# Scatters of a mixture of experts that wait tile by tile

## The reference

```
x = x + attention_like(conditioning(x, fside))      # two-way recurrences, gates, W_out
x = x + mixture_of_experts(conditioning2(x, fside)) # what this case is about
```

```
probs = softmax(xr @ Wg);  gate_vals, expert_idx = top_k(probs, 2)
h = relu(einsum('ecd,edf->ecf', dispatched, w1))    # 512 -> 2048
expert_out = einsum('ecf,efd->ecd', h, w2)          # 2048 -> 512
out[row] = sum over its two experts of gate * expert_out
```

## Time and profile before

| what | us |
|---|---|
| median of 3 runs | 1220.02 (1217.79 to 1220.59) |
| profiled execution, its device time | 1219.18 |
| its span, first to last instruction | 1217.1 |
| PE busy | 1039.4 (85% of the span) |
| PEld busy | 827.9 (68%) |
| DVE busy | 677.7 (56%) |
| ACT busy | 533.8 (44%) |
| POOL busy | 322.6 (27%) |
| PE clock granted, mean | 0.953 of full |

### The profile page before, as it was taken

One profiled execution on the slowest core, in us unless ns is written; L12 is line 12 of the kernel. 1 busy time (PEld: TensorE's weight loads), 2 busy tenths in 40 slices (PEclk: granted clock), 3 DMA queues, 4 the chain that ended last, 5 costly groups with the idle time before them and its releaser, 6 DMA issues.

```text
span 1217.1 us, 17595 instructions
## 1 busy us (share of the span) xinstructions
PE 1039.4 (85%) x5058; PEld 827.9 (68%) x5059; DVE 677.7 (56%) x970; ACT 533.8 (44%) x914; POOL 322.6 (27%) x251
## 2 busy tenths in 40 slices
PE   1146797787799829999999999999999999999994
PEld 0022344344348529998999899989898888999883
DVE  6989899899781523334333433355555344343553
ACT  5455746826844212334333433344545334333453
POOL 3878818648630330001100200020201101100302
PEclk9998998997999759999999999999999999999998
DMA  5251340211010452113421621282535234322711
GB/s 191 104 166 35 122 133 35 69 70 69 0 71 35 174 175 104 69 69 118 106 69 69 149 76 69 69 220 91 186 138 186 83 132 134 87 69 69 216 70 21
DMA packets 63406, 125.29 MB, mean 103 GB/s; under 512 B 4726, under 2 KB 4762, under 8 KB 63384
## 3 DMA queue, kind: packets, MB, share of 16 engines
q1 hardware_dynamic: 54728, 107.91, 25.6%
q0 software_dynamic: 8656, 17.13, 7.0%
HBM read 93.04 MB, written 35.22 MB: 105 GB/s over the span
## 4 chain that ended last, share of the span: by engine, by line
PE 58%; issue 1%; ACT 1%; DVEq 1%; DVE 1%; POOL 0%; ACTq 0%; POOLq 0%
PE ps_y L1137 10%; PE ps_y L1138 10%; PE ps_y L1139 10%; PE ps_h L1117 9%; PE ps_h L1119 9%; PE ps_h L1118 9%; PE ps_t L1087 1%; POOL out_dram L1066 0%; ACT xh L1232 0%; ACT y L1239 0%; DVEq L1177 0%; DVE hl L1294 0%; ACT w1h L1204 0%; DVE w1l L1255 0%; ACTq L1177 0%
## 5 line engine op out<-in xcount | busy, mean ns | idle before, releaser
L1117 PE MATMUL ps_h<-xh,w1h 128*128 128x320 f32 (+3 forms) x768 | 247.6, 322 | 7.9 <-issue 4.0
L1119 PE MATMUL ps_h<-xh,w1l 128*128 128x320 f32 (+3 forms) x768 | 243.6, 317 | 0.0
L1118 PE MATMUL ps_h<-xl,w1h 128*128 128x320 f32 (+3 forms) x768 | 243.5, 317 | 0.0
L1066 POOL DMA_INDIRECT out_dram<-y,token x40 | 64.6, 1615 | 657.6 <-ACT y L1239 487.7
L1294 DVE SCALAR_TENSOR_TENSOR hl<-ps_h,hh 128x320 fp32r<-128x320 f32 (+1 forms) x192 | 106.9, 558 | 194.0 <-ACT hh L1228 185.3
L1137 PE MATMUL ps_y<-w2h,hh 128*128 128x512 f32 x528 | 206.5, 391 | 1.9 <-DVE hl L1294 1.9
L1138 PE MATMUL ps_y<-w2h,hl 128*128 128x512 f32 x528 | 206.7, 391 | 0.0
L1139 PE MATMUL ps_y<-w2l,hh 128*128 128x512 f32 x528 | 206.1, 390 | 0.0
L1258 DVE TENSOR_TENSOR w2l<-raw,w2h 128x512 fp32r<-128x512 f32 x128 | 88.6, 692 | 196.5 <-ACT w2h L1207 193.6
L1228 ACT ACTIVATE hh<-ps_h 128x320 fp32r<-128x320 f32 (+1 forms) x192 | 94.4, 492 | 232.4 <-PE ps_h L1119 232.2
L1207 ACT ACTIVATE w2h<-raw 128x512 fp32r x128 | 80.7, 631 | 211.2 <-PE ps_y L1139 210.2
(11 more groups left out here) (194 smaller groups left out, 1290.4 us busy)
## 6 DMA issues: line engine op xcount, KB each, us to landing
raw<-in_L_ffn_w_dram SPq DMA_DIRECT2D x64, 1024.0 KB
slots<-r_rows SPq DMA_DIRECT2D x8, 1302.5 KB, 16.1
rows<-slots SPq DMA_DIRECT2D x8, 1302.5 KB
f_rows<-in_fside_BxSxS_dram SPq DMA_DIRECT2D x5, 1024.0 KB, 5.3
rows<-in_x_dram SPq DMA_DIRECT2D x4, 1024.0 KB, 6.4
out_dram<-x_rows SPq DMA_DIRECT2D x4, 1024.0 KB, 4.9
slots<-r_rows POOLq DMA_DIRECT2D x1, 1302.5 KB
rows<-slots SPq DMA_DIRECT2D x5, 260.5 KB, 4.1
```

Of the source, the lines that this page charges most:

```text
L1117: nc.tensor.matmul(o, w1h[:, j, dt, :], xh[:, dt, lo:hi], start=(dt == 0), stop=False)
L1118: nc.tensor.matmul(o, w1h[:, j, dt, :], xl[:, dt, lo:hi], start=False, stop=False)
L1119: last = nc.tensor.matmul(o, w1l[:, j, dt, :], xh[:, dt, lo:hi], start=False, stop=(dt == CT - 1))
```

## The change

Every eviction now raises its engine's semaphore by one. The thresholds are scaled: `Y_EVEN` = 3 even tiles and `Y_ODD` = 2 odd tiles per expert. In a narrow expert, whose tile 4 has no eviction, ScalarE's eviction of tile 2 adds 2. GpSimd waits, ahead of scatter i, for the count that tile i's eviction reaches; the wait for `s_y0` (y has been cleared) comes first. TensorE and VectorE wait for the same events as before, under the new thresholds.

```diff
+    Y_EVEN, Y_ODD = (ST + 1) // 2, ST // 2
...
-            pool.wait_ge(s_ya, e + 2)
-            pool.wait_ge(s_yv, e + 2)
             pool.wait_ge(s_y0, 1)
-            pool.nop(nofuse=True)
             for i in range(ST):
+                if i % 2 == 0:
+                    pool.wait_ge(s_ya, Y_EVEN * (e + 1) + i // 2 + 1)
+                else:
+                    pool.wait_ge(s_yv, Y_ODD * (e + 1) + i // 2 + 1)
+                pool.nop(nofuse=True)
                 pool.indirect_dma_start(
...
-                    pe.wait_ge(s_ya, e + 1)
-                    pe.wait_ge(s_yv, e + 1)
+                    pe.wait_ge(s_ya, Y_EVEN * (e + 1))
+                    pe.wait_ge(s_yv, Y_ODD * (e + 1))
...
-        act.sem_inc(s_ya, 1)
+        act.sem_inc(s_ya, Y_EVEN)
...
                 for i in range(0, ST if wide else ST - 1, 2):
-                    last = a.activation(y[:, i], ps_y[:, i, :], ACT.Copy, scale=gate[:, i:i + 1])
-                last.then_inc(s_ya, 1)
+                    a.activation(y[:, i], ps_y[:, i, :], ACT.Copy, scale=gate[:, i:i + 1]).then_inc(
+                        s_ya, 2 if i == ST - 3 and not wide else 1)
...
-        dve.sem_inc(s_yv, 1)
+        dve.sem_inc(s_yv, Y_ODD)
...
-            dve.wait_ge(s_ya, e + 1)
-            dve.wait_ge(s_yv, e + 1)
+            dve.wait_ge(s_ya, Y_EVEN * (e + 1))
+            dve.wait_ge(s_yv, Y_ODD * (e + 1))
...
                 for i in range(1, ST if wide else ST - 1, 2):
-                    last = v.tensor_scalar(y[:, i], ps_y[:, i, :], gate[:, i:i + 1], None, ALU.mult)
-                last.then_inc(s_yv, 1)
+                    v.tensor_scalar(y[:, i], ps_y[:, i, :], gate[:, i:i + 1], None, ALU.mult).then_inc(s_yv, 1)
```

## The result

The changed kernel takes 1216.76 us (median of 22 runs, 1215.48 to 1219.51), the kernel before 1218.95 (22 runs, 1217.45 to 1220.93). Ratio 0.9985, 95% interval 0.9978 to 0.9992: faster, by 1.0 to 2.7 us, so the gain is clear of the noise though it is only 0.2%. Forecast were 1218.8 us and a gain of 1.2.

What follows compares the result with a forecast made beforehand. TensorE was taken to bound the expert stage and GpSimd's scatters the tail. The first scatter's 1.19 us, all other terms 0, off the 1220.02 us median gave 1218.8 us, range 1217.2 to 1220.7.

Steps and rivals of the forecast that it cites:

- What bounds it, and that only the tail counts: Whole kernel: TensorE alone sets the expert stage, GpSimd's five scatters the end from 1203.2 us; only there can time be gained.
- The wait of 648 us: Experts' first scatters waiting for evictions, 487.7 us behind ScalarE and 160.2 behind VectorE; nearly all idle time beside 728 us of matmuls.
- The first scatter, 1.19 us: Last expert: waiting for tile 0 alone, GpSimd starts scattering at 1202.02 us in place of 1203.21, 1.19 us earlier.
- Scatters two to five: Last expert: each follows at a pitch of 1.86 us with its tile ready; none waits again.
- the added waits: Four more waits and empty instructions between GpSimd's scatters: cost taken 0, at worst 2.1 us.
- register arithmetic: Scaled thresholds on PE, VectorE and GpSimd: some 0.1 us per expert, covered by other waits, cost 0.
- increments: Semaphore raises on every eviction, carried by instructions already there: cost 0.
- The boundaries: Seven changes of expert: the scatter comes about 1.15 us earlier, TensorE gains nothing.
- the gate copy: Rival at seven changes of expert: VectorE's copy shut out by an earlier scatter, 1.20 us each, total 1227.2 us; chance 0.05.
- the collision that I looked for: VectorE's copy falling inside GpSimd's earlier scatter between experts and standing back 1.20 us each time; chance 0.05.
- the median of the runs shown, 1220.02, is 0.84 above the profiled one; on it the sum gives 1218.8 us: Whole kernel: the 1.19 us gain taken off the median of three runs, 1217.79 to 1220.59 us, giving 1218.8.

Runs made afterwards that it cites:

- before with padded code: The kernel before, plus a long-satisfied wait and an empty instruction ahead of each of an expert's five scatters; 1219.37 us, ratio 1.0006.

## Why the prediction missed

- *What bounds it, and that only the tail counts*: right. The wait of 648 us is still there in the trace of the changed kernel (648.9 us, now all behind ScalarE), and it costs nothing.
- *The first scatter, 1.19 us*: right, 1.23 measured. The scatter follows the end of the first eviction by 0.83 us (1200.17 - 1199.34), not 0.87.
- *Scatters two to five, the added waits, register arithmetic, increments*: right, all at 0. I had bounded the waits by 2.1 us; sixteen pairs of them still hide. Their price in the sequencer was half of what I used in the experiments' expectation.
- *The boundaries, the gate copy*: right that it costs nothing in this kernel. A copy inside a scatter runs on. But the collision that I looked for existed in another form. Where evictions end earlier, an early scatter goes with a load of a count by VectorE that is up to 0.76 us longer, at 4 of 7 boundaries. The changed kernel escapes it: its scatters start 0.4 us ahead of the gate copy at the last boundary and not 1.9, and all its loads behind a boundary take 0.31 to 0.33.
- *The step that failed* is "the median of the runs shown, 1220.02, is 0.84 above the profiled one; on it the sum gives 1218.8 us", with its range of 1.5 us either way (down to 1217.3; it is written as 1217.2). Two of those three runs were long ones; over 22 runs before takes 1218.95, so 1.07 of the 2.04 us by which the forecast is too high is the base. The other 0.97 is the difference of the medians, 2.19 in place of 1.19 (0.03 is rounding). The mechanism was right and the base and the spread were mis-sized. The traces give 0.04 of that to the tail. The rest goes with how often the low clock came ahead of 455 us: in the profiled pair that alone was 1.57 us. At like clock the gain is 1.3. Whether the rarer low-clock runs are chance or follow from the program stays open. Counted by their time, the changed kernel had them in 6 of 34 runs (above 1218.2 us), before in 41 of 100 (above 1219.4), and before with padded code in 6 of 12.

## What to carry over

Before a wait is split, ask which of its instances ends on the path: here one of eight, and its price is read from two rows, the eviction that it waits for and the one that it could wait for. A gain of 1 us under a spread of 3 us between runs can be forecast only as a difference; put the base on many runs, or give the range the whole spread of those there are. And when a DMA is started earlier, look at what it will run beside, small loads of a sequencer included.

## What the runs showed of the hardware

- A scatter by GpSimd (1.55 us) is held back by VectorE: at its start by a subtraction of two SBUF tensors or a copy that is running (by what is left of it less 0.12 us), and at its end by a copy alone (it ended 0.12 us behind it). VectorE was never held back (1.48 to 1.50 us for each of the twelve). An eviction from PSUM beside it did not matter (1.57 us beside one, and 1.57 without in the tail of before).
- A load of one number from SBUF by VectorE's sequencer takes 0.31 to 0.33 us. It took 0.53 to 1.14 in the eight cases where it began 2.2 us after the start of an expert's first scatter, mostly ahead of that scatter's first row. Why is open.
- GpSimd's sequencer runs ahead of the engine through 17 waits per scatter, each with an empty instruction (about 0.06 us a pair): the gaps between scatters stay 0.30 us.
